# First norm and first attention in one block, rows normalised one per slot, constants in padding columns only

## What is computed

```python
x = x + tanh(g_xattn[0]) * L0_xattn(layernorm(x), ctx, Wq, Wk, Wv, Wo, bo)     # heads of 64
x = x + tanh(g_ffn[0])   * L0_ffn(layernorm(x), w_gate, w_up, w_down)          # quantised
x = x + tanh(g_xattn[1]) * L1_xattn(layernorm(x), ctx, mask, wq, wk, wv, wo)   # heads of 16
x = x + tanh(g_ffn[1])   * L1_ffn(layernorm(x), ...)                           # shared + top 2 of 8 experts
layernorm: (x - mean) / sqrt(var + 1e-5);  attention: softmax(q k^T * scale) v, then Wo and a bias
```

## Time and profile before

| what | value |
|---|---|
| median of 3 runs | 1660.81 us (1658.57 to 1665.26) |
| the profiled execution | 1660.71 us, span 1658.9 us |
| PE busy | 1402.6 us (85%), 15436 instructions |
| DVE busy | 1237.2 us (75%) |
| ACT busy | 1107.8 us (67%) |
| POOL busy | 210.1 us (13%) |
| mean granted clock of TensorE | 0.936 |

### The profile page before, as it was taken

How to read it: one execution, slowest core, us unless ns; L and a number is a source line. 1 busy time by engine, 2 the same in 40 slices (tenths; PEclk the granted TensorE clock), 3 DMA queues, 4 the chain that set the end, 5 groups by cost and what they waited for, 6 DMA issues and landing times. The chain is left out here.

```text
span 1658.9 us, 40477 instructions
## 1 busy us (share of the span) xinstructions
PE 1402.6 (85%) x15436; PEld 998.6 (60%) x15436; DVE 1237.2 (75%) x3092; ACT 1107.8 (67%) x2445; POOL 210.1 (13%) x185
## 2 busy tenths in 40 slices
PE   1699999999999996294186989898988879999996
PEld 1466766677666665252174666666666557788884
DVE  6478888887888886949767999889888877344443
ACT  5467777777777774257516888888888744366663
POOL 4501000000010000400003000000000010034443
PEclk9999999999999999598597999999999979999998
DMA  4122323322323221000010212121010072212221
GB/s 146 56 62 93 108 90 97 96 84 83 109 83 115 74 71 42 29 1 26 0 56 11 82 48 80 52 76 34 18 34 12 5 252 65 63 32 49 46 47 23
DMA packets 64911, 105.69 MB, mean 64 GB/s; under 512 B 7434, under 2 KB 38899, under 8 KB 63571
## 3 DMA queue, kind: packets, MB, share of 16 engines
q1 hardware_dynamic: 58002, 94.83, 18.2%
q0 software_dynamic: 6720, 8.27, 3.1%
HBM read 68.88 MB, written 35.11 MB: 63 GB/s over the span
## 5 line engine op out<-in xcount | busy, mean ns | idle before, releaser
L1326 ACT ACTIVATE a_p<-a_s,a_nb 112x375 f32<-112x375 f32 x256 | 140.9, 598 | 26.6 <-DVE a_nb L1440 26.3
L294 PE MATMUL a_ps_o<-a_vh,a_pt 125*128 125x64 f16 (+1 forms) x1536 | 152.7, 183 | 2.7 <-ACT a_pt L1339 0.8
L1247 PE MATMUL a_ps_t<-ident,a_p 112*128 112x112 f32 x768 | 117.0, 282 | 42.8 <-ACT a_p L1326 41.7
L296 PE MATMUL a_ps_o<-a_vh,a_pt 125*128 125x64 f16 (+1 forms) x1536 | 151.1, 182 | 0.0
L295 PE MATMUL a_ps_o<-a_vl,a_pt 125*128 125x64 f16 (+1 forms) x1536 | 151.0, 182 | 0.0
L583 ACT ACTIVATE a_p<-a_ps_s,a_nb 112x375 f32<-112x375 f32 x256 | 143.8, 572 | 3.5 <-DVE a_scaled L674 3.5
L591 ACT ACTIVATE a_pt<-a_ps_t 125x336 f16<-125x336 f32 x256 | 101.8, 448 | 66.1 <-PE a_ps_t L522 65.7
L294 PEld LDWEIGHTS a_ps_o<-a_vh,a_pt 125*128 125x128 f16 x1536 | 133.4, 97 | 14.9 <-ACT a_pt L1339 6.7
L1247 PEld LDWEIGHTS a_ps_t<-ident,a_p 112*128 112x128 f32 x768 | 78.8, 144 | 97.5 <-issue 82.6
L295 PEld LDWEIGHTS a_ps_o<-a_vl,a_pt 125*128 125x128 f16 x1536 | 130.7, 98 | 11.0
L1440 DVE CUSTOM_DVE_ANT_0 a_s<-a_s,a_fill 112x375 f32<-112x375 f32 x256 | 129.9, 545 | 5.5
(11 more groups left out here) (428 smaller groups left out, 4544.9 us busy)
## 6 DMA issues: line engine op xcount, KB each, us to landing
a_piece<-in_w SPq DMA_DIRECT2D x72, 256.0 KB, 3.1
split_weights<-a_pair SPq DMA_DIRECT2D x72, 256.0 KB, 3.4
w<-split_weights SPq DMA_DIRECT2D x8, 1024.0 KB, 6.1
a_ctx<-in_ctxT SPq DMA_DIRECT2D x16, 375.0 KB, 3.7
ctx<-a_cx SPq DMA_DIRECT2D x16, 375.0 KB, 4.4
a_cx<-ctx SPq DMA_DIRECT2D x16, 375.0 KB, 5.8
w1h<-split_weights SPq DMA_DIRECT2D x2, 1792.0 KB, 14.0
w1l<-split_weights SPq DMA_DIRECT2D x2, 1792.0 KB, 16.4
```

The lines of the kernel that those rows point to most:

```text
L294: nc.tensor.matmul(out, wh, mh, start=(i == 0), stop=False)
L296: last = nc.tensor.matmul(out, wl, mh, start=False, stop=(i == n - 1))
L1247: mm = nc.tensor.matmul(ps_t[:, 2 * (g % 2) + i, t * S:(t + 1) * S], p32[:, g % 2, i, t * KV:t * KV + 128], ident32[0:S, 0:S], start=(t == ...
L1326: nc.scalar.activation(p32[:, g % 2, i, 0:NC], s2[:, g % 2, i, :], ACT.Exp, bias=nb[:, g % 2, i:i + 1], scale=-1.0).then_inc(exp_done, 1)
```

## The change

The setup and the first norm have no block of their own any more; `attention0_phase` does their work, and norm_phase is left for the feed forward.

- SP loads the first context, Wk, rows 0 to 3 of x, Wq, the gates, Wv, the small vectors, rows 4 to 15, Wo. There are four staging buffers in place of three.
- A weight's high part is one ACT operation with the scale in it, its low part one DVE operation. Wo is split in slots 1 and 2.
- FIRST holds K0 to K7, Q0, Q1 and X0, X1 of rows 0 to 3. JOBS_0 holds the rest. xn holds four rows. The statistics of rows 4 to 15 stand in slots 3 to 5, their square root in slot 6, their reciprocal in slot 7; the normalised rows stand in twelve slots (ROW_AT) and their X jobs in six (X_AT), in batches 1, 2, 4, 5, 8 and 9.
- The bias additions move into POOL's loop over the batches, one a batch; W waits for its own.
- POOL sets only the padding columns of qh, ql, p32 and pt. own and neg16 are made here once and kept for the second attention.
- In the second attention DVE sets the padding of vl, vh, qh and ql behind the normalised rows, POOL that of p32 and pt.

```diff
+                  [("K5", 1), ("K6", 1)]]
+        ROW_AT = {NP * b + p: TG * n + i for n, b in ((1, 1), (2, 4), (3, 8))
+                  for i, (b, p) in enumerate(((b, 2), (b, 3), (b, 6), (b + 1, 2)))}
+        X_AT = {NP * b + p: (f"X{k}", n) for n, b in ((1, 2), (2, 5), (3, 9)) for k, p in enumerate((3, 6))}
         JOBS = [[("V00", 0), ("V01", 0)], [("V02", 0), ("K7", 0), ("K0", 1)], [("OT1", -1), ("Q0", 1), ("K1", 1)],
                 [("W", -1)], [("V10", 0), ("V11", 0)], [("V12", 0), ("K2", 1)], [("OT0", 0), ("K3", 1), ("Q1", 1)],
                 [("K4", 1), ("K5", 1), ("K6", 1)]]
...
@@ -411,9 +402,31 @@
 
         @block.sync
         def _(sp):
+            def load_weight(i):
+                src, hi, lo = loads[i]
+                wait(sp, w_lo, i - (SB - 1))
+                sp.dma_start(stage[:, i % SB, 0:hi.free_size()].rearrange("p (a b) -> p a b", a=src.shape[1]),
+                             src).then_inc(w_in[i % SB], 16)
+
+            def load_rows(t0, t1, landed):
+                sp.dma_start(x_res[:, t0:t1, :], A["x"].rearrange("(t p) d -> p t d", p=S)[:, t0:t1, :]
+                             ).then_inc(landed, 16)
+
             sp.dma_start(ctx32[:], A["ctxT"][:, :, 0:NC].rearrange("k p n -> p k n")).then_inc(ctx_in, 16)
+            for i in WK:
+                load_weight(i)
+            load_rows(0, TG, x_in[0])
+            for i in WQ:
+                load_weight(i)
+            for i, name in enumerate(("g_xattn", "g_ffn")):
+                sp.dma_start(gates[:, 2 * i:2 * i + 2], A[name].partition_broadcast(128)).then_inc(g_in, 16)
+            for i in WV:
+                load_weight(i)
             sp.dma_start(bo[:], A["L0_xattn_bo"].partition_broadcast(S)).then_inc(bo_in, 16)
             sp.dma_start(nw[:], A["norm_wT"]).then_inc(nw_in, 16)
+            load_rows(TG, B, x_in[1])
+            for i in WO:
...
                     pe.wait_ge(ctx_lo, b + 1)
+                if (name, b) == ("K0", 0):
+                    pe.wait_ge(w_lo, WK[1] + 1)
+                if (name, b) == ("Q0", 0):
+                    pe.wait_ge(w_lo, WQ[1] + 1)
+                    pe.wait_ge(job_lo, NUMBER["X1", 0] + 1)
+                if (name, b) == ("V00", 0):
+                    pe.wait_ge(w_lo, WV[1] + 1)
+                if (name, b) == ("W", 0):
+                    pe.wait_ge(w_lo, WO[1] + 1)
+                if name == "Q0" and b % TG == 0 and b > 0 and NUMBER["X1", b // TG] + 1 > i - 1:
+                    pe.wait_ge(job_lo, NUMBER["X1", b // TG] + 1)
+                if name == "X0":
+                    pe.wait_ge(normed, TG * (b + 1))
+                if (name, b) == ("X0", 0):
+                    pe.wait_ge(id_made, 2)
                 if name == "OT0":
                     pe.wait_ge(o_ready, 2 * b + 1)
                 if name == "OT1":
...
+
             act.wait_ge(ctx_in, 16)
             nc.scalar.activation(cx[:, 0, 0, :, :], ctx32[:], ACT.Copy).then_inc(ctx_hi, 1)
+            for i in WK:
+                weight_high(i)
+            high("K0", 0)
+            roots(1, 0, TG)
+            high("K1", 0)
+            for i in WQ:
+                weight_high(i)
+            high("K2", 0)
+            high("K3", 0)
+            act.wait_ge(g_in, 32)
+            nc.scalar.activation(tanh_g[:], gates[:], ACT.Tanh).then_inc(tanh_done, 1)
+            act.wait_ge(zeroed, 4)
+            for name, b in FIRST[4:6]:
+                high(name, b)
...
+                if g == 6:
+                    roots(2, TG, B)
                 for i in slot_pieces(g):
                     split_high(i)
 
         @block.gpsimd
         def _(pool):
-            for buffer in (qh, ql, pt, p32):
-                nc.gpsimd.memset(buffer[:], 0.0).then_inc(zeroed, 1)
-            pool.wait_ge(bo_scaled, 1)
-            for b in range(B):
+            for m in (ident32, ident16):
+                nc.gpsimd.memset(m[:], 0.0).then_inc(id_zeroed, 1)
+            pool.wait_ge(id_zeroed, 2)
+            for m in (ident32, ident16):
+                nc.gpsimd.affine_select(out=m[:], in_=m[:], compare_op=ALU.not_equal, fill=1.0, base=0,
+                                        pattern=[[-1, 128]], channel_multiplier=1).then_inc(id_made, 1)
+            nc.gpsimd.memset(own[:, 0:1], 0.0).then_inc(own_made, 1)
+            nc.gpsimd.memset(own[:, 1:2], 1.0).then_inc(own_made, 1)
+            pool.wait_ge(id_made, 2)
+            nc.gpsimd.tensor_scalar(neg16[:], ident16[:], -1.0, 0.0, ALU.mult, ALU.add).then_inc(own_made, 1)
+            pool.wait_ge(own_made, 3)
+            for n, value in enumerate((1.0, 0.0)):
+                for r in range(4):
+                    nc.gpsimd.memset(own[32 * r:32 * r + DH1, n:n + 1], value).then_inc(own_made, 1)
+                pool.wait_ge(own_made, 3 + 4 * (n + 1))
+            for buffer in (qh, ql):
+                nc.gpsimd.memset(buffer[:].rearrange("p c h s -> p (c h) s")[:, :, S:], 0.0).then_inc(zeroed, 1)
+            nc.gpsimd.memset(p32[:].rearrange("p r i n -> p (r i) n")[:, :, NC:], 0.0).then_inc(zeroed, 1)
+            nc.gpsimd.memset(pt[:].rearrange("p r i a t s -> p (r i a t) s")[:, :, S:], 0.0).then_inc(zeroed, 1)
...
 
         @block.vector
...
+            def reciprocal_roots(n, t0, t1):
+                r, e = rstd[:, t0:t1], near[:, t0:t1]
+                dve.wait_ge(std_ready, n)
+                stat(nc.vector.reciprocal(r, std[:, t0:t1]))
+                stat(nc.vector.tensor_tensor(e, r, r, ALU.mult))
+                stat(nc.vector.tensor_tensor(e, e, var[:, t0:t1], ALU.mult))
+                stat(nc.vector.tensor_scalar(e, e, -0.5, 1.5, ALU.mult, ALU.add))
...
+                weight_low(i)
+            dve.wait_ge(x_in[0], 16)
+            stat(statistics(0, TG))
+            variances(0, TG)
+            low("K0", 0)
+            reciprocal_roots(1, 0, TG)
+            for t in range(TG):
+                normalise_row(t)
+            low("K1", 0)
+            for i in WQ:
+                weight_low(i)
+            low("K2", 0)
+            low("K3", 0)
+            dve.wait_ge(zeroed, 4)
+            for name, b in FIRST[4:6]:
+                low(name, b)
+            for i in WV:
+                weight_low(i)
+            for name, b in FIRST[6:]:
+                low(name, b)
             dve.wait_ge(bo_in, 16)
+            dve.wait_ge(tanh_done, 1)
             nc.vector.tensor_scalar(bo_g[:], bo[:], tanh_g[0:S, 0:1], None, ALU.mult).then_inc(bo_scaled, 1)
             link(nc.vector.tensor_scalar(gate[:], tanh_g[0:S, 0:1], 1.0 / (WS * WS), None, ALU.mult))
-            dve.wait_ge(zeroed, 4)
-            for name, b in FIRST:
-                low(name, b)
-            dve.wait_ge(bo_added, B)
             for g in range(SLOTS):
                 js = slot_jobs(g)
                 if g < G:
...
@@ -719,6 +863,19 @@
                     normalise(g - 2)
                 for name, b in js[1:]:
                     low(name, b)
+                if g in (1, 2):
+                    weight_low(WO[g - 1])
+                if g == 3:
+                    dve.wait_ge(x_in[1], 16)
+                if 3 <= g < 6:
+                    last = statistics(TG * (g - 2), TG * (g - 1))
+                if g == 5:
+                    stat(last)
+                    variances(TG, B)
+                if g == 7:
+                    reciprocal_roots(2, TG, B)
+                if g in ROW_AT:
+                    normalise_row(ROW_AT[g])
                 for i in slot_pieces(g):
                     split_low(i)
 
...
@@ -1363,17 +1517,8 @@
 
         @block.gpsimd
         def _(pool):
-            nc.gpsimd.memset(own[:], 0.0).then_inc(own_made, 1)
-            pool.wait_ge(own_made, 1)
-            for r in range(4):
-                nc.gpsimd.memset(own[32 * r:32 * r + DH1, 0:1], 1.0).then_inc(own_made, 1)
-            pool.wait_ge(own_made, 5)
-            nc.gpsimd.tensor_scalar(own[:, 1:2], own[:, 0:1], -1.0, 1.0, ALU.mult, ALU.add).then_inc(own_made, 1)
-            nc.gpsimd.memset(vl[:], 0.0).then_inc(zeroed, 1)
-            nc.gpsimd.memset(vh[:], 1.0).then_inc(zeroed, 1)
-            for buffer in (qh, ql, p32, pt):
-                nc.gpsimd.memset(buffer[:], 0.0).then_inc(zeroed, 1)
-            nc.gpsimd.tensor_scalar(neg16[:], ident16[:], -1.0, 0.0, ALU.mult, ALU.add).then_inc(zeroed, 1)
+            nc.gpsimd.memset(p32[:].rearrange("p r i n -> p (r i) n")[:, :, NC:], 0.0).then_inc(zeroed, 1)
+            nc.gpsimd.memset(pt[:].rearrange("p r a i t s -> p (r a i t) s")[:, :, S:], 0.0).then_inc(zeroed, 1)
             pool.wait_ge(bo_scaled, 1)
             for b in range(B):
                 pool.wait_ge(normed, b + 1)
...
@@ -1465,9 +1610,12 @@
             link(nc.vector.tensor_tensor(rstd[:], rstd[:], near[:], ALU.mult))
             for t in range(TG):
                 normalise_row(t)
+            for buffer, value in ((vl, 0.0), (vh, 1.0)):
```

(47 more changed lines are left out.)

98 lines of the change are left out of this document (57 added, 41 removed), and 3 rows, old and new, of the table JOBS_0.

## The result

The changed kernel takes 1623.6 us (median of 4 runs, 1622.6 to 1625.3) against 1660.5 (4 runs, 1658.6 to 1665.3) for the one before: a ratio of 0.977, 95% interval 0.975 to 0.978. The prediction was 1620.0, range 1608 to 1637. The profiled execution has a span of 1622.2 us against 1658.9, so 36.7 us are to be found in the traces. TensorE's busy time is 1399.8 us, where it was 1402.6: the change took no work away, it filled holes.

What follows compares the result with a forecast made beforehand. The kernel was taken to be TensorE's own work with holes in it. The terms 23.2 + 9.3 - 4 + 10.2 + 2 = 40.7 us, off 1660.7, gave 1620 us, range 1608 to 1637.

Steps and rivals of the forecast that it cites:

- The start: Start of the first attention: scores of slot 0 at 31.5 us against 54.7, 23.2 us earlier.
- my two cases: Before slot 0: K7 done at 29.8 us with the clock up early, or 32.6 with it low until Q1.
- Slots 0 to 7: First batch of the first attention: 46.3 us before, 37 after, a gain of 9.3 us.
- the 37 us for the batch: Length taken for slots 0 to 7, between 33 and 41 us, as TensorE and VectorE wait for each other.
- X jobs: Batches 1 to 9: six X jobs add 2.8 us of TensorE work and 1.2 of handshakes, minus 4 us.
- Second attention: Start of the second attention: first scores at 872.4 us and not 882.6, 10.2 us gained.
- The 2 us that I hoped for from a clock that stays up: First slots of the second attention: a clock that stays up more gains 0 to 4 us, taken as 2.
- Half filled: Rival: VectorE becomes the bound in FIRST and slots 3 to 5, holes half filled; 1635 us, chance 0.17.
- POOL's stall belongs to the first tensor operation anywhere: Rival at the second attention's start: the 9.33 us stall may move elsewhere, no second gain; 1632 us, chance 0.06.
- late weights: Rival at the start: transfers share the engines, Wk lands at about 12 us, 5 later; 1625 us, chance 0.08.
- The slower case: Rival: waits in batch 0 keep TensorE at 1.2 GHz; batches 0 and 1 wholly low give 1687 us, chance 0.02.
- my signs of being wrong: Stall before X0, batch 0 over 41 us, clock below 1.00 past slot 2, or 10 us wait before second attention's Q.

Runs made afterwards that it cites:

- e1: The changed kernel with the second attention as before: own and neg16 made again there on POOL, six whole buffers set; 1633.1 us.
- e9: The changed kernel with the twelve aggregates spread over slots 4 to 6, and square root and reciprocal one slot later; 1622.5 us.
- e10: e9 with the square root of rows 4 to 15 in slot 11 and the first two rows of each group two slots later; 1626.3 us.
- e7: The changed kernel with all rows of x queued ahead of the context and Wk; 1628.6 us.
- e6: The changed kernel with the first attention's four buffers set whole by POOL instead of padding columns only; 1625.1 us.
- e11: e10 with K1's low part ahead of the four normalised rows, and K2 and K3 ahead of Wq's halves; 1623.8 us.
- e12: e9 with e11's order of the first jobs before slot 0; 1623.8 us.
- e4: The kernel before with only padding columns set in the second attention; own and its tensor_scalar stay there on POOL; 1653.1 us.
- e3: The kernel before with own and neg16 made in the setup block; the second attention's six whole-buffer memsets stay; 1656.6 us.

## Why the prediction was right, and where it was off

- *The start.* Forecast 23.2, measured 23.8. The chain of the forecast came nearly as walked: context at ScalarE at 4.28 (4.5), first K matmul at 9.76 (9.5), K1's low part done at 16.72 (16.2), Wq's low halves at 18.98 (18.6), slot 0 at 30.89 (31.5). Some of the closeness is luck: with the same code up to slot 0, e1, e9 and e10 have the first K matmul at 10.32, 10.40 and 10.51 and slot 0 at 31.45, 32.10 and 30.76. The clock did neither of my two cases: it rose at about 12.5 us, after 2.8 us of K matmuls, was low again by K4 at 21.87, and rose again in Q0. e7 shows that the path starts at Wk's landing: 5.7 us later there, 5 us at the end. VectorE's low halves of Wk cost 1.22 to 1.23 us each, 1.2 forecast. e6 bears out that the constants are hidden.
- *Slots 0 to 7.* Forecast 9.3, measured 6.5. The step that was off is the 37 us for the batch, which took 39.8. My lower bounds (TensorE 30.5, VectorE 32.7) stand, and in e9, without the table loads, the batch took 36.7. What the 37 put at nothing is the loads and the clock: 1.7 us for the two loads in slot 7, and 1.3 for a granted clock of 0.76 in that slot, 0.55 until 67.0. I had written that the loads sit in one slot, and yet added them only to ScalarE's sum. For the table loads, the next activation again starts 0.02 us behind a load (64.22, 65.52), so the Trainium skill's drain of 1.38 us (ScalarE: Activation LUTs, What ACT_TABLE_LOAD costs) is not in these rows. By this rule the loads cost 5.3 us, by the rows 2.6; TensorE lost 1.7.
- *X jobs.* Forecast -4, measured -2.9: the three batches that hold two of them take 37.7 us and not 36.74, 0.97 a pair, which is TensorE's own 0.94. The 1.2 us of handshakes that I added were not there. The last batch gave 1.6 back with a clock of 1.00 where it was 0.93, so the row of the table reads -1.3.
- *Second attention.* Forecast 10.2 to its first scores, measured 9.9. The 2 us that I hoped for from a clock that stays up did not come: the clock is 0.65 from 846 to 870 and the rest of the program took 1.1 us longer. So the term is nothing at best; the 1.1 us lie inside the spread of 5 us between executions, so its sign isn't shown. The account of the 3.6 us by which the forecast was under: slots 0 to 7 2.8, this term 3.1, the feed forward 1.1 and the second hole 0.3 too little gain, against 0.6 more at the start and 2.7 less lost after slot 8. Together that is 4.0 for the profiled execution, which lies 0.4 above the median.
- *The rivals.* Half filled (1635) had the right mechanism for batch 0: VectorE is the bound of slot 6, busy 6.71 of 6.81 us. But that was within my 37; what exceeded it had another cause. That POOL's stall belongs to the first tensor operation anywhere is refuted by e1, late weights by the first K matmul at 9.76, and by the order seen in e7. The slower case had its condition for one slot: one of my signs of being wrong, a clock below 1.00 past slot 2, came in slot 7 (0.76) and cost 1.3 us. It didn't last, and from slot 8 on the window shows 1.00.

Open: why the granted clock in the second attention differs by 0.02 between executions, why a low stretch falls in slot 7, in slot 1 or (in e9, e11 and e12) in neither, why Wk's second piece lands up to 1.2 us later, and what made the feed forward's stretch 1.1 us longer. Counted from the end of the last W, that stretch takes 200.8 to 202.7 us in the fourteen traces (201.4 before, 202.5 in the changed kernel), and no experiment has an edit there.

## What to carry to other kernels

A phase boundary is priced by what the first instruction of the bound engine has to have, not by the work of the phase: put the loads in the order in which that engine needs them, begin with jobs that need the fewest of them, and let the rest ride in slots. Constants that buffers need belong in columns that nobody writes, and once: that brought 7 us where VectorE and ScalarE waited for the memsets (e4), and nothing that shows where they were hidden (e6). When small work is spread over slots, place it by the fullest engine of each slot: a pair of table loads made the loop 1.7, 1.8 or up to 2.4 us longer by its slot. Before a difference of 1 us is put down to an edit, look whether executions with the same code up to that point differ as much.

## What was not expected

POOL stood 9.3 us before its first tensor operation of the second attention, in e1 9.07, in e4 9.32, but 0 at the start of the program. The kernel before has a second such row: 6.96 us before the tensor_tensor that follows the partition_all_reduce of the second norm. All come behind a PARTITION_ALL_REDUCE with nothing but memsets between; memsets themselves were not held up. What holds POOL isn't shown.

```profile
687.51 2.71 POOL L232 PARTITION_ALL_REDUCE n_amax<-n_amax  x1 [11.49 <-DVE n_amax L208]
...
697.17 5.51 POOL L1031 TENSOR_TENSOR qw_q<-qw_q,qw_bscale 128x1536 f32<-128x1536 f32 x2 [6.96 <-issue]
...
820.04 0.35 POOL L841 PARTITION_ALL_REDUCE f_am<-f_mx  x1 [30.47 <-DVE f_mx L924]
```

In the changed kernel the additions after the second attention's start are the first such operation, and they start 0.09 us after the operation that releases them, 13.5 us into the block: whatever holds POOL was over by then.

```profile
845.04 3.09 POOL L1525 TENSOR_TENSOR x_res<-x_res,a_bo_g 112x256 f32<-112x256 f32 x4 [13.02 <-DVE a_bo_g L1625]
```

And memsets on POOL hold some of VectorE's operations, not all that work in SBUF. The tensor_scalars were held: bias_q takes 8.50 us and not 0.35, four normalised rows 6.20 and not 1.38 (e3). Beside the same memsets e3's tensor_tensors of 112x16 took 0.18 us (0.17 to 0.18 in the changed kernel without them), its sixteen aggregates 1.17 (1.17), and e6's low halves of Wk 1.23. The Trainium skill (SBUF — State Buffer, Who interferes with whom) says that a tensor_scalar can run in a mode that takes a port pair shared with GpSimd, and that whoever issues first has the pair for the whole instruction and the other waits. By this rule a held row ends where a memset ends. The trace agrees: in e3 the first two rows end at 863.06 and 864.09, the memsets of qh and ql at 862.91 and 863.95, and the third row ends at 868.15, the last memset at 868.00. But one instruction is not the measure of the wait: the third row sat through two memsets, and bias_q through all six.
